# A six-stage batch pipeline on one core: the rolled loop over batches, against the same loop written out on every engine

## What is computed

```python
x = x + tanh(g_xattn[0]) * L0_xattn(layernorm(x), ctx)      # 4 heads, softmax, output projection
x = x + tanh(g_ffn[0])   * L0_ffn(layernorm(x))             # linear plus a low-rank term
x = x + tanh(g_xattn[1]) * L1_xattn(layernorm(x), ctx, ctx) # one head
x = x + tanh(g_ffn[1])   * L1_ffn(layernorm(x))             # 16-head self attention + top 2 of 8 experts
```

## Time and profile before

| what | value |
|---|---|
| median of 3 runs | 922.59 us (921.9 to 923.68) |
| the profiled execution's own time | 922.53 us |
| its span, first to last instruction | 920.5 us |
| mean granted TensorE clock | 0.978 |
| PE busy | 838.9 us (91%), 11764 matmuls |
| DVE, ACT, POOL busy | 677.8 us (74%), 609.9 us (66%), 518.1 us (56%) |

### The profile page before, as it was taken

How to read it: one execution, slowest core, us unless ns; L and a number is a source line. 1 busy time by engine, 2 the same in 40 slices (tenths; PEclk the granted TensorE clock), 3 DMA queues, 4 the chain that set the end, 5 groups by cost and what they waited for, 6 DMA issues and landing times. The chain is left out here.

```text
span 920.5 us, 34780 instructions
## 1 busy us (share of the span) xinstructions
PE 838.9 (91%) x11764; PEld 667.1 (72%) x11764; DVE 677.8 (74%) x1622; ACT 609.9 (66%) x1358; POOL 518.1 (56%) x891
## 2 busy tenths in 40 slices
PE   3688999999999999999999999999999999998875
PEld 1467777777777777787777777777777787776653
DVE  2677877877877787778777877877787778777553
ACT  2555777776677776666777776677677666777543
POOL 3323656555665665555556555665665555555544
PEclk9879999999999999999999999999999999999988
DMA  6412222121112221212222111122221212211100
GB/s 208 157 50 66 70 78 78 60 66 58 58 61 75 75 75 54 63 49 71 65 75 75 62 65 58 56 61 75 75 75 54 64 51 69 65 59 56 38 6 11
DMA packets 41290, 61.88 MB, mean 67 GB/s; under 512 B 6158, under 2 KB 28036, under 8 KB 41128
## 3 DMA queue, kind: packets, MB, share of 16 engines
q1 hardware_dynamic: 41256, 61.43, 21.3%
HBM read 37.77 MB, written 3.67 MB: 45 GB/s over the span
## 5 line engine op out<-in xcount | busy, mean ns | idle before, releaser
L1328 POOL TENSOR_TENSOR acc<-part,acc 112x256 f32<-112x256 f32 x256 | 188.7, 737 | 70.4 <-DVE acc L1148 51.6
L1244 POOL TENSOR_SCALAR ln_ve<-ln_mv 112x1 f32<-112x1 f32 x128 | 50.6, 396 | 197.1 <-DVE ln_mv L979 191.6
L1248 POOL TENSOR_TENSOR ln_rs<-ln_ve,cst 112x1 f32<-112x1 f32 x128 | 136.4, 1065 | 10.7
L822 ACT ACTIVATE part<-bankE,cgS 112x256 f32<-112x256 f32 x256 | 107.4, 473 | 20.3 <-POOL cgS L1311 14.0
L331 PE MATMUL bankE<-wexs_hi,xT_hi 128*112 128x512 f16 x256 | 98.6, 385 | 7.7 <-ACT part L822 4.0
L331 PE MATMUL bankE<-wexs_hi,xT_lo 128*112 128x512 f16 x256 | 97.0, 379 | 0.0
L331 PE MATMUL bankE<-wexs_lo,xT_hi 128*112 128x512 f16 x256 | 96.9, 379 | 0.0
L829 ACT ACTIVATE xn<-x,ln_sh,ln_rs 112x256 f32<-112x256 f32 x96 | 57.6, 600 | 52.9 <-POOL ln_sh L1251 52.1
L1073 DVE TENSOR_TENSOR p_lo<-p2T,p_hi 112x896 f16<-112x896 f32 x64 | 67.5, 1096 | 7.4 <-ACT p_hi L813 7.4
L1115 DVE TENSOR_REDUCE mx<-quad 112x8 f32<-112x896 f32 x64 | 69.5, 1087 | 1.0
L1007 DVE TENSOR_TENSOR p_lo<-p0T,p_hi 125x896 f16<-125x896 f32 x64 | 54.5, 854 | 21.4 <-ACT p_hi L750 21.4
(11 more groups left out here) (240 smaller groups left out, 3357.5 us busy)
## 6 DMA issues: line engine op xcount, KB each, us to landing
ctf<-in_ctx_T SPq DMA_DIRECT2D x32, 375.0 KB, 3.3
ctn<-in_ctx_n SPq DMA_DIRECT2D x32, 375.0 KB
kvB<-kvA SPq DMA_DIRECT2D x32, 281.2 KB, 2.4
kc<-kvB SPq DMA_DIRECT2D x32, 187.5 KB
xin<-in_x SPq DMA_DIRECT2D x32, 112.0 KB, 2.0
x<-in_x SPq DMA_DIRECT2D x32, 112.0 KB, 2.1
out_x<-xout SPq DMA_DIRECT2D x32, 112.0 KB, 3.0
wex<-in_w_exp SPq DMA_DIRECT2D x1, 2048.0 KB, 10.0
```

The costliest lines, as they stand in the source:

```text
L822: act.activation(part[:, e, :], bankE[0:LQ, n * D:(n + 1) * D], ACT.Identity, scale=cgS[:, e:e + 1])\
L1244: pool.tensor_scalar(ln_ve[n][:], ln_mv[n][:, 1:2], EPS, None, ALU.add).then_inc(ln[n].sem, 1)
L1248: pool.tensor_tensor(ln_rs[n][:], ln_ve[n][:], minus_half, ALU.pow).then_inc(ln[n].sem, 1)
L1328: pool.tensor_tensor(acc[:], part[:, 2 * j + n, :], acc[:], ALU.add).then_inc(moe_sum[j].sem, 1)
```

## The change

`PEEL` goes, and all 37 iterations are called with plain numbers, on all five engines. No step and no order of steps changes. The whole diff:

```diff
@@ -20,7 +20,6 @@
 DMA = 16
-PEEL = 6
@@ -226,11 +225,7 @@
         def iterations(eng, body):
-            for i in range(PEEL):
-                body(*at(i))
-            with eng.Fori(PEEL, NB) as i:
-                body(i, i - 1, i - 2, i - 3, i - 4, i - 5)
-            for i in range(NB, NB + STAGES - 1):
+            for i in range(NB + STAGES - 1):
                 body(*at(i))
@@ -313,10 +308,8 @@
-            for i in range(PEEL):
+            for i in range(NB - 1):
                 body(*at(i), True)
-            with sp.Fori(PEEL, NB - 1) as i:
-                body(i, i - 1, i - 2, i - 3, i - 4, i - 5, True)
             for i in range(NB - 1, NB + STAGES - 1):
                 body(*at(i), False)
```

## The result

The changed kernel took 931.43 us, median of 4 runs (929.41 to 938.2). The kernel before took 922.47 us beside it (4 runs, 921.9 to 923.68). The ratio is 1.0108, with a 95% interval of 1.0056 to 1.0161: slower by 1.1%, where 917.7 us was forecast. The profiled execution of after took 932.19 us.

The account below looks back on a forecast made before the run. The period was bound by PE's work from `norm_T(2)` to `scores0` plus a chain through DVE, POOL and ACT. 26 x (0.16 + 0.19 - 0.11) = 6.2 us gained, less 1.3 for code loads, gave 917.7 us; range 908 to 926.

Parts of the forecast that it names:

- The three gains and losses on the cycle of PE, DVE and POOL: Per iteration: 0.16 us gained before `project_q`, 0.19 at PE's iteration head, 0.11 lost where DVE and POOL instructions meet.
- its branch and registers: Head of PE's iteration, from `out0_T` to `scores1`: removing PE's loop branch and register work gains 0.19 us.
- Loading the code: Straight-line code streaming over DMA queues: SP stops and delayed copies cost 1.3 us in all, bounds nothing to 5.2.
- One of three loads meets them in about a quarter of the iterations: Copies to B, in flight some 2.4 of 26.5 us: how often a code load coincides with one.
- Holds one back by 1.0 us at most.: SP's copies: a code load sharing a DMA engine delays one by at most 1.0 us, of which 0.18 is spare.
- the low end: Code-load cost taken as 1.3 us, near the lower bound, as one straight-line iteration's copy reached POOL only 0.03 us later.
- less 0.18 us: Wait of POOL for SP's copy to B: 0.18 us of lateness to spare before it costs anything.
- SP's path takes over: Rival, cycle through SP's copies and POOL: slower from 0.42 us mean delay; 929.8 us at 0.7; chance 0.17.
- The better meeting: Rival, DVE and POOL around `rstd(2)`: iterations 0.59 us shorter than the loop's, total 907.2 us; chance 0.12.
- no gain at all: Rival, chain before `norm_T(2)`: it takes back whatever PE wins, total stays 922.5 us; chance 0.18.
- a load at every branch back: Rival, PE's loop branch: each turn refetches its head, so 26 loads of 1.0 us would go, 896.5 us; chance 0.03.

## Why the prediction was wrong

**Right: what the loop cost.** The three gains and losses on the cycle of PE, DVE and POOL (0.16, 0.19 and -0.11 us, together 0.24) came to 0.27, and the 26.28 us of a clean iteration shows it. The sum is right in part by luck, as the split is not. PE's form alone is worth 0.09 us in both pairs that isolate it (26.36 against 26.27, 26.54 against 26.45), where its branch and registers were put at 0.19. The other engines' is worth 0.18, where 0.16 less 0.11, so 0.05, was written. Why half of the gap at PE's head does not reach the period wasn't tried.

**Wrong: the term "Loading the code", 1.3 us, with 5.2 as its upper bound.** It was 15.9 us in the profiled run, 0.64 us an iteration where 0.05 was taken. Three parts of that step failed:

- *How often.* "One of three loads meets them in about a quarter of the iterations" took the loads as scattered, and counted the flight of the copy to B alone. But five copies go out of `kvB` first, and the copy to B waits for the last. The loads of the nine slowest iterations started from 4.2 to 7.4 us, only one of them in the flight of the copy to B, and 16 of the 25 iterations are longer than 26.4 us.
- *How much.* "Holds one back by 1.0 us at most." A load of about 1 us held back the issue of the copy by up to 1.7 us (8.77 us into one iteration instead of 7.04), and where a load on queue 14 met the late copy, up to 1.2 us more in landing came on top. Over the 25 iterations the issue is 0.52 us later than in a clean one (7.57 for 7.05), and from there to POOL it takes 0.19 us more (2.86 for 2.67).
- *The evidence.* I drew the low end from one straight-line iteration where the copy was 0.03 us late. That iteration has its three loads at 0.8, 12.6 and 21.9 us, all clear of the copies (in after at 0.8, 12.7 and 21.4). And the 0.03 us compared only the time from issue to POOL: by the same rows this copy was issued 121.54 - 114.18 = 7.36 us into its iteration, where the loop has 6.96. Three loads an iteration on queue 8 was right (queue 14 has 60 packets and not about 90), but that they move was not looked for, and one iteration could not show it.

What held is how lateness passes on: in full, less 0.18 us, by the prediction. With L1312 at 9.7 us the period is 26.27, at 10.4 26.82, at 10.9 27.37, at 11.3 27.92 and at 12.3 28.51: POOL 0.66, 1.18, 1.56 and 2.53 us later makes it 0.55, 1.10, 1.65 and 2.24 us longer, and on average 0.71 makes 0.64. So the mechanism, loads that hold SP's copies back and POOL with them, was written down; its size was not.

**The rival that came true** is "SP's path takes over", with a chance of 0.17. It put the turning point at a mean delay of 0.42 us, and gave 26.82 us and 929.8 us for a mean of 0.7. In after POOL's L1312 starts 10.43 us into the iteration on average, 0.71 later than in a clean one, and the mean period is 26.906. Its sign to look for also came: idle time of L1312 for the copy over 1.3 us (67.0 us in 28 waits, 2.4 each, against 36.6 and 1.3 before). The better meeting, no gain at all, and a load at every branch back did not come.

**Branches and crossings.** Queue 8 had 21 packets in before and in both kernels with PE looped, so PE's branch back costs no load here. The Trainium skill (Runtime: NRT & Kernel Launch, "Instruction fetch mechanics") gives a stall at a taken branch out of a window of two blocks as one reason why kernels prefer full unrolling. Against this, PE's loop of 751 instructions, three blocks of 256, ran its 26 turns without a load; it fits the 2048 instructions that the same section gives for PE's instruction memory. The section's other half, that a crossing is mostly hidden, holds for PE itself (mean period 26.303 with all loads and two buffers). It leaves out the engine's neighbours: here all of the cost is theirs.

## What to carry to other kernels

Writing this loop out bought 0.27 us per iteration, where registers and branches stood on the cycle that sets the period, and paid with code that streams in over the DMA engines. Before doing it, find the transfers whose landing decides the period, read their slack, and count instructions per iteration against 16 KB loads to see whether the loads drift through them; one clean iteration proves nothing. If a chain of copies has little slack, decouple it first (here a second buffer, 0.5% faster than before in either form). In this kernel the form of PE's loop then made no measurable difference.

## What the runs showed of the hardware

- Loads of code delay other transfers: the last packet of the copy waited until the load's 0.96 us were over. Three loads of 16 KB an iteration, the first of them 6.4 us into it and not 0.9, make the difference between 28.10 and 26.36 us, with the same code in the loop.
- A load of 0.96 us on one of 16 engines can start what comes out as 2.2 us of period: the next copy was issued 1.46 us late, and landed 1.1 us later still with a load of another engine's code in its flight.
- POOL's instructions take twice as long beside DVE's (two L1321 3.17 us for 1.52), but of the 4.5 us by which `rstd(3)` was late, 2.2 were left at PE.
- Empty increments on PE are hidden where one follows a matmul (17 an iteration, 26.29 us for 26.27), but 171 in front of the program put off the first scores2 by 12.2 us, and four between two matmuls moved these from 0.31 to 0.60 us apart.
- The first scores2 comes at 88 or at 92 us in different executions, the kernel being the same in front of it (88.23 before, 88.54 after; 92.67 with PE looped), and the granted clock from 20 to 40 us was 0.83 in the first two and 0.74 in the third. Much of the spread within one kernel (917.88 to 924.17 us for PE looped) is of this size. What decides it stayed open.
